# First attention's softmax sums by 32x32 transposes on VectorE, and three weight requests at other steps

## What is computed

```python
qkv = x @ Wqkv.T;  scores = causal(q @ k.T / sqrt(128))
x = layernorm(x + (softmax(scores) @ v) @ out_w.T)
# second: Q, K with scaled columns, V from x @ Wa; the same softmax; @ Wp
x = layernorm(x + attn2(x) @ Wp)
```

## Time and profile before

| | us |
|---|---|
| median of 3 runs | 1966.73 |
| lowest | 1963.15 |
| the profiled execution | 1965.32 |
| its span on the slowest core (6) | 1963.8 |
| first attention, head 0 to the final matmuls (core 6) | about 97 to 573 |
| second attention with its projections | about 790 to 1725 |
| TensorE, VectorE, ScalarE, GpSimd busy | 1907.4, 1135.3, 965.5, 253.9 |

### The profile page before, as it was taken

One profiled execution on the slowest core, in us unless ns is written; L12 is line 12 of the kernel. 1 busy time (PEld: TensorE's weight loads), 2 busy tenths in 40 slices (PEclk: granted clock), 3 DMA queues, 4 the chain that ended last, 5 costly groups with the idle time before them and its releaser, 6 DMA issues.

```text
span 1963.8 us, 30387 instructions; the slowest of 8 cores (1951.1 to 1963.8 us)
## 1 busy us (share of the span) xinstructions
PE 1907.4 (97%) x10286; PEld 992.5 (51%) x10286; DVE 1135.3 (58%) x1976; ACT 965.5 (49%) x1333; POOL 253.9 (13%) x372
## 2 busy tenths in 40 slices
PE   5999999999999999999999999999999999889997
PEld 2445445544444444555647465564746556334443
DVE  0288889988953644145556556555565655524333
ACT  0288888888853433144453545445354444622221
POOL 3011111111122441001010001100000000100000
PEclk9999999999999999999999999999999999999999
DMA  9712121221487996132121322212122220593642
GB/s 144 125 33 57 41 65 41 58 49 39 87 163 138 274 280 167 41 55 54 34 49 31 62 44 55 54 33 51 34 58 44 54 44 17 84 201 107 224 184 86
DMA packets 91271, 170.01 MB, mean 87 GB/s; under 512 B 39544, under 2 KB 58096, under 8 KB 81904
## 3 DMA queue, kind: packets, MB, share of 16 engines
q1 hardware_dynamic: 61936, 107.77, 19.4%
q0 software_dynamic: 28896, 59.77, 19.3%
q10 hardware_dynamic: 288, 0.52, 0.1%
HBM read 185.62 MB, written 33.80 MB: 112 GB/s over the span
## 4 chain that ended last, share of the span: by engine, by line
PE 92%; DMA 4%; ACT 1%; DVE 1%; issue 1%; POOL 1%; DVEq 0%; ACTq 0%; POOLq 0%; SPq 0%
PE pj L319 32%; PE c_ps L671 11%; PE s_ps L441 11%; PE pj L1149 11%; PE s_ps L951 11%; PE pj L951 5%; PE c_ps L951 3%; PE l_ps L951 3%; DMA bufA<-wp 2%; DMA bufB<-xT 2%; PE l_ps L576 1%; PE s_ps L823 1%; PE pj L406 1%; ACT pt L453 0%; PE pj L650 0%
## 5 line engine op out<-in xcount | busy, mean ns | idle before, releaser
L453 ACT ACTIVATE pt<-s_ps,mbias 128x1024 bf16<-128x1024 f32 (+2 forms) x640 | 630.7, 988 | 465.9 <-PE s_ps L441 390.2
L319 PE MATMUL pj<-bufA,ws 128*128 128x512 bf16 x2048 | 479.9, 379 | 1.0 <-DVE z L974 1.0
L671 PE MATMUL c_ps<-pt,v 128*128 128x512 bf16 (+3 forms) x1280 | 341.9, 349 | 5.7 <-ACT cf L685 4.0
L319 PEld LDWEIGHTS pj<-bufA,ws 128*128 128x128 bf16 x2048 | 198.3, 98 | 230.9 <-issue 3.8
L510 DVE TENSOR_TENSOR acc<-acc,pt 128x1024 f32<-128x1024 f32 x180 | 219.8, 1221 | 69.8 <-ACT pt L453 65.5
L319 PE MATMUL pj<-bufB,ws 128*128 128x512 bf16 x896 | 243.5, 379 | 0.1
L1149 PE MATMUL pj<-wv,bufA 128*128 128x256 bf16 x2048 | 238.3, 273 | 0.0
L461 POOL TENSOR_SCALAR_AFFINE_SELECT pt<-pt 128x256 bf16<-128x256 bf16 x256 | 124.7, 489 | 872.3 <-ACT pt L453 857.5
L1149 PEld LDWEIGHTS pj<-wv,bufA 128*128 128x128 bf16 x2048 | 199.4, 98 | 37.5 <-issue 0.3
L979 ACT ACTIVATE sqs<-z 128x512 f32<-128x512 f32 x128 | 80.5, 629 | 240.0 <-DVE z L974 230.9
L671 PEld LDWEIGHTS c_ps<-pt,v 128*128 128x128 bf16 x1280 | 124.2, 98 | 141.9 <-issue 19.6
(11 more groups left out here) (141 smaller groups left out, 1857.1 us busy)
## 6 DMA issues: line engine op xcount, KB each, us to landing
rb<-rr_res SPq DMA_DIRECT2D x116, 256.0 KB, 3.8
ws<-wqk POOLq DMA_DIRECT2D x32, 512.0 KB, 6.3
z<-x SPq DMA_DIRECT2D x16, 1024.0 KB, 6.5
x_res<-z SPq DMA_DIRECT2D x16, 1024.0 KB, 7.6
z<-x_res SPq DMA_DIRECT2D x16, 1024.0 KB, 6.5
out<-z SPq DMA_DIRECT2D x15, 1024.0 KB, 7.4
bufB<-xT POOLq DMA_DIRECT2D x16, 512.0 KB, 39.3
bufB<-wo POOLq DMA_DIRECT2D x4, 2048.0 KB, 25.6
```

The lines of the kernel that those rows point to most:

```text
L319: tok = P.pe(lambda t, c=c, b=b: t.matmul(pj[b][:, :], lhs(c), rhs(c), start=(c == 0), stop=(c == NCH - 1)), waits=wt, inc=(c == NCH - 1))
L453: self.exp_tok[g] = P.ac(lambda s: s.activation(pt[:, 0:n], sp[:, 0:n], AF.Exp, bias=mbias[h % 2][:, :]), waits=[self.s_tok[g], self.mb_ok ...
L671: last = t.matmul(c_ps[:, q0:q0 + n], self.vbuf(h)[:, c * 128:(c + 1) * 128], pt[:, o:o + n], start=(beg and n_ == 0), stop=(end and n_ == 1))
```

## The change

Attention 1 gets a scratch tile `tr1` in the room of a hi and a lo tile, and is built with `turned` set, so that it goes through `turn`, `lsum_turned` and the short `recip`. `split_hi`, `split_lo`, `lsum` and the long reciprocal are deleted. In attention 1, `lsum_turned` comes at step 23, that is step 3 of the next head; the reciprocal stays at step 4 of the next head. Where attention 1 calls `sums` (before `feed`) is kept, now by the flag `fold_out`.

The copy that begins window 0 in attention 1 moves from VectorE to ScalarE. The last head's windows 2 and 3 of attention 1 are copied from PSUM to the room of `acc`, not to the ring `cf`. Quarters 1, 2 and 3 of Wp are requested at steps 4, 8 and 12.

```diff
-    hi1 = [row("hi1_0", 36864, 512, BF16), row("hi1_1", 24576, 512, BF16)]
-    lo1 = [row("lo1_0", 37888, 512, BF16), row("lo1_1", 25600, 512, BF16)]
+    tr1 = row("tr1", 36864, 512, F32)
...
                 if kind == "a":
-                    t1 = P.ve(lambda v: v.tensor_copy(src, pt[:, 0:512]),
-                              waits=[ok, self.src_read[0]] +
-                              ([] if self.fold_out else [self.fold_ok[NW - 1]]))
+                    if self.fold_out:
+                        t1 = P.ac(lambda s: s.copy(src, pt[:, 0:512]),
+                                  waits=[ok, self.src_read[0]])
+                    else:
+                        t1 = P.ve(lambda v: v.tensor_copy(src, pt[:, 0:512]),
+                                  waits=[ok, self.src_read[0], self.fold_ok[NW - 1]])
...
                 free = [self.cf_free[m]] if m is not None else \
-                    [self.turn_ok, self.norm_tok[(H - 3, NW - 1)]]
+                    [self.turn_ok, self.fold_ok[NW - 1], self.norm_tok[(H - 3, NW - 1)]]
...
         def add_up(self, g, n, todo):
-            for what, hh, w in todo:
-                if what == "split" and not self.turned:
-                    self.split_hi(w)
             if g + 1 < n:
                 self.sums(g + 1)
             for what, hh, w in todo:
                 if what == "split":
-                    (self.turn if self.turned else self.split_lo)(w)
+                    self.turn(w)
...
     at1 = Att("a1", 0, lambda h: kT, lambda h: q1[h % 2], lambda h: v1, bufA, pt1, acc1, f1,
-              True, hi1, lo1, cf1, rb1, None, r41, (3, 7, 13, 21), (8, 10, 15, 23), 4,
-              (6, 7, 8, 12), (10, 12, 14, 16))
+              True, [], [], cf1, rb1, None, r41, (3, 7, 13, 21), (0, 0, 0, 23), 4,
+              (6, 7, 8, 12), (10, 12, 14, 16), tr1,
+              [None, None] + [row(f"cl1_{i}", 32768 + 2048 * i, 512, F32) for i in range(2)])
...
-    at2.at_step[(H - 1) * NST + 7] = lambda tok: wp_tok.append(
-        load_big(bufA, wp_d, 1, [x2_end[0], tok]))
-    at2.at_step[(H - 1) * NST + 13] = lambda tok: wp_tok.extend(
-        load_big(bufA, wp_d, i, [x2_end[0], tok]) for i in (2, 3))
+    for n, ew in ((4, 1), (8, 2), (12, 3)):
+        at2.at_step[(H - 1) * NST + n] = lambda tok, ew=ew: wp_tok.append(
+            load_big(bufA, wp_d, ew, [x2_end[0], tok]))
```

More of the change, by code:

```diff
@@ L527, in sums @@
                                        waits=[t] + ([self.src_read[1]] if self.fold_out else []))
-        def split_hi(self, w):
-            src, _ = self.sources(w)
-            hi = self.hi[w % len(self.hi)]
-            self.hi_ok[w] = P.ac(lambda s: s.copy(hi[:, :], src),
-                                 waits=[self.fold_ok[w], self.hl_free[w % len(self.hi)]])
-        def split_lo(self, w):
-            src, n = self.sources(w)
-            hi, lo = self.hi[w % len(self.hi)], self.lo[w % len(self.hi)]
-            self.lo_ok[w] = P.ve(lambda v: v.tensor_sub(lo[:, :], src, hi[:, :]),
-                                 waits=[self.hi_ok[w], self.fold_ok[w],
-                                        self.hl_free[w % len(self.hi)]])
-            self.src_read[n] = self.lo_ok[w]
         def turn(self, w):
@@ L564, in lsum_turned @@
             self.hl_free[0] = self.l_tok[h]
-        def lsum(self, h, w):
-            hi, lo = self.hi[w % len(self.hi)], self.lo[w % len(self.hi)]
-            def mm(t):
-                last = None
-                for half in (0, 1):
-                    n = 2 * w + half
-                    band = strip[:, 112 - 16 * n:240 - 16 * n]
-                    for src in (hi, lo):
-                        last = t.matmul(l_ps[:, 0:256], band, src[:, half * 256:half * 256 + 256],
-                                        start=(n == 0 and src is hi),
-                                        stop=(n == 2 * NW - 1 and src is lo))
-                return last
-            self.l_tok[h] = P.pe(mm, waits=[self.hi_ok[w], self.lo_ok[w], tok_strip] +
-                                 ([self.r_tok.get(h - 1), bank_free[7]] if w == 0 else []))
-            self.hl_free[w % len(self.hi)] = self.l_tok[h]
         def recip(self, h):
@@ L593, in recip @@
                 return
-            self.r_tok[h] = P.ve(lambda v: v.reciprocal(self.r4[:, 0:256], l_ps[:, 0:256]),
-                                 waits=[self.l_tok[h], self.ro_tok.get(h - 1)])
-            self.ro_tok[h] = P.dma(
-                "sync", f"{self.tag}ro",
-                rr_d[self.row0 + h, :, :].rearrange("w (a c) -> (w a) c", a=2),
-                self.r4[0:128:16, 0:256], waits=[self.r_tok[h]])
         def rbuf(self, h, w):
@@ L731, in run @@
                 todo = plan.get(g, [])
-                if not self.turned:
+                if self.fold_out:
                     self.add_up(g, n, todo)
@@ L743, in run @@
                 self.feed(target(h, i))
-                if self.turned:
+                if not self.fold_out:
                     self.add_up(g, n, todo)
@@ L748, in run @@
                 for what, hh, w in todo:
-                    if what == "lsum" and not self.turned:
-                        self.lsum(hh, w)
-                    elif what == "lsum":
+                    if what == "lsum":
                         self.lsum_turned(hh)
```

## The result

The change made the kernel slower by 0.2%: ratio 1.0022, interval 1.0013 to 1.0031. The median of 14 executions is 1970.7 us (lowest 1966.5) against 1965.6 (lowest 1963.1) for the kernel before in the same series of runs. Some executions of each kernel, 6 of the 14 of the changed one, ran in a slower state of the chip, and the ratio is of the others alone, whose median is 1968.5 us for the changed kernel. The forecast was 1961, with a range that holds 1970.7, but it had the sign wrong: some 4 us more came where some 4 less were forecast. The profiled execution of after took 1966.5 us, the shortest of the 14.

A forecast was written before the change was run, and what follows sets the result against it. The prediction took TensorE as the first attention's bound, VectorE 10% under it, and late Wp weights as the final projection's stall. It summed 1965.3 + 1.0 (first attention) - 5 (Wp requests) to 1961 us, range 1950 to 1975.

The forecast's parts named there:

- The bound changes hands: First attention: VectorE, needing 30.35 us a head, replaces TensorE as the bound, whose need falls from 30.4 to 28.7.
- The price on VectorE: First attention: 4.8 us of VectorE work go out and 6.7 come in, net +1.9 us a head.
- The waits that remain: First attention: VectorE as the bound still waits 0.4 us a head, giving period 30.75 and +2.7 us over 13 periods.
- The row of 530 to 545 us: Head 14 of the first attention: VectorE busy 14.02 of 15 us, 0.5 us of waits; source of the 0.4 a head.
- cost 0: First attention, window 0 copy moved to ScalarE: the exponential queued behind it delays nothing; without that cover 1.3 us a head.
- Head 0, head 14, tail: First attention outside the 13 periods: head 0 -1.3 us, head 14 +0.6, tail -1.0 from the shorter reciprocal.
- the hole of 75 GB/s at 1704 to 1708: DMA traffic before the final projection: filling it with earlier Wp requests is worth 2 to 4 us, 3.5 taken.
- the limit of 39 us: Whole kernel: a 2% change in time, about what a measurement can tell from none; slower 0.03, faster 0.02, same 0.95.
- B: First attention: TensorE stays the bound, added VectorE work fits into its waits, 28.7 to 29 us a head; 1938 us, chance 0.07.
- A: First attention: VectorE keeps 2.09 us of waits a head and TensorE's clock falls after stalls; 1983 us, chance 0.15.
- C: Final projection: earlier Wp requests change nothing, bandwidth alone sets quarter 2's landing; -1 us or so, 1965, chance 0.2.
- D: Final projection: the Wp stall goes wholly, 9 us, with VectorE never waiting in the first attention; 1952 us, chance 0.13.

The follow-up runs named there:

- the run with late normalisations: Kernel before with Wp requests at steps 4, 8, 12 and head 14's products in attention 2's last head at steps 8, 10, 13, 15: ratio 1.0005.

## Why the prediction went wrong, point by point

The forecast was +1.0 us for attention 1 and -5 for the requests. Alone, the attention measured +5.7 and the requests -2.2. So both terms failed, the attention's by 4.7 us and the requests' by 2.8.

**The bound changes hands: right.** TensorE is busy for 94.8% of the stretch (382.10 of 403.08), VectorE for 92.2%, and TensorE stands for results that hang on VectorE. Taking 2.7 us a head from VectorE shortened the period by 1.27.

**The price on VectorE: right.** Forecast 28.45 + 1.9 = 30.35 us a head; measured (403.08 - 10.0) / 13 = 30.24, so 1.8 were added. The durations taken from attention 2 hold: 703 for the transpose, 686 for the sum, 343 for the reciprocal.

**The waits that remain: the failed step in attention 1.** Forecast 0.4 us a head, measured 10.0 / 13 = 0.77, which alone is 13 x 0.37 = 4.8 us; less 1.4 for the smaller need, that is 3.4, and core 0's stretch of 403.1 is 3.3 over the forecast of 399.8 (the median core's 402.5 is 2.7 over). The row of 530 to 545 us was the right kind of row, but it was read from a kernel in which the copy was on VectorE. With the copy there the waits are 4.9 / 13 = 0.38, just the forecast value, but the need is 30.79, so that the forecast period of 30.75 is met in neither kernel. The forecast gave the copy on ScalarE "cost 0" and so took its move as a saving of 0.6 us a head; the saving that remains is 0.15. It argued from ScalarE's 328 of 397 us, an average. That ScalarE stands 1.0 us for the mask in the diagonal steps, with the exponential of the next step behind it, is measured; that this makes VectorE's waits is the likely reason and not shown.

**Head 0, head 14, tail: 1.7 us of gains that didn't come.** Head 14 was forecast at +0.6 and came at +0.4 and +0.6. The tail stayed at 20.5 us to the tenth, so the shorter reciprocal in front of the early tile sat on no path. For head 0 the first reciprocal moves by -0.8 us on the later and -0.3 on the earlier cores, and its medians lie between 122.0 and 126.8 in all kernels with either head 0: a gain of 1.3 can't be seen, nor excluded. In all attention 1 and its tail cost 5.7 us instead of 1.0.

**Wp: the failed step in the requests.** The forecast read the hole of 75 GB/s at 1704 to 1708 as room, "which goes on beside the four broadcasts of reciprocals". It filled the hole with quarter 1, which was to bring quarter 2 forward by 3.5 us, and priced the early tile and the mask as the only ones that could suffer. Both halves of that failed. Quarter 2 came forward by nothing on the later cores (55.8 us after the last short reciprocal before and after) and by 0.7 on the earlier ones. And the broadcasts suffered. They then took a median of 11.6 us instead of 6.3, and the first reader stands in VectorE's in-order stream ahead of the reciprocal for which TensorE waits: +4.1 and +4.2 us in the last head. The row of the hole says itself that there was less room than its GB/s suggest: the share of the DMA engines is 0.76 there, against 1.13 with the full queue. The Trainium skill (DMA: Bandwidth & Descriptors, Queues, rings and completion order) says that each DMA engine serves its queues in turn by packets. By that rule a second 2 MB transfer beside them slows the broadcasts though they are on SyncE's queue; the trace shows the later landing, and no run here shows the order of the packets. A hole still stands in after, with 100 GB/s and a share of 0.77 at 1709 to 1713 on core 0, where the broadcasts now are, so the early request didn't fill it, and what makes it stays open.

The size of the stall was right by luck: forecast 2.8, measured 2.43 on core 0, and -5.9 us in the final part of the later cores where -5 was forecast. But the stall fell because TensorE came 4.1 us later and not because the weights came sooner, and with the last head at its old length the stall is back at 6.1 us (the run with late normalisations). On the later cores the two together are -5.9 + 4.1 = -1.8 us, on the earlier ones, which had 1.9 to 2.7 us to win, -2.5 + 4.2 = +1.7.

**Sum.** By the stages the later cores change by -0.8 + 5.7 + 0.4 + 4.1 - 5.9 = +3.5 us, and their spans by +4.2; the sums of medians don't close better than that. The forecast spoke of even and odd cores as if the odd ones were early by nature; they were so in one execution. The slowest core went from 1963.8 to 1964.9 in the profiled executions; the ratio of the runs is 0.22%, or 4.3 us.

**Small sums.** For the requests the forecast's own numbers give 2.8 + 1.7 = 4.5 us left of 8.9 (6.34 + 2.57), so -4.4 and not -5. Four quarters of 2 MB at 148 GB/s from 1688.2 end near 1745 and not 1747. And neither case named for the limit of 39 us reaches it: 3 us of waits a head are 13 x (33.35 - 30.54) = +36.5 us before the gains of 1.7 and 5, and B with all of Wp is -21 - 1.7 - 9 = -32.

**Rivals.** A fell: VectorE's waits for the mask were 7.8 us, not 20.8, and the clock stayed at 1.00 in the 13 heads, so that its price of a stall in each head was never put to the test. B fell: 1.8 us didn't fit into 2.1 of waits. C came nearest for the requests: it said -1 us, they gave -2.2, and its reason, that bandwidth sets the landing, is what the landings show. D is seen on single cores (no stall for Wp on cores 1, 2, 4, 5 and 6) and shows that the stall's end isn't a gain by itself.

## What to carry to other kernels

When work moves to an engine that is within 10% of the bound, its price can be read well from rows of the same operation elsewhere, to 0.1 us in 1.9 here; the waits that remain can't be read from a stretch in which another engine still has a job that the change moves, and an engine's average load doesn't say that an instruction which stands behind a wait costs nothing.
A transfer that is asked for earlier doesn't land earlier for that: compare its landing, counted from a fixed instruction, before you credit a shorter stall to it, for a reader that comes later sees a shorter stall too.
A hole in the DMA traffic is not free room if small transfers run in it: before asking for a large one earlier, list the small ones in flight, and follow each to its reader and to what stands behind that reader in order.
With unequal cores, compare those that ended late with those that ended late, whatever their number, and never count two halves as averaged between two engines until a run shows that a surplus is carried over.

## What the runs showed of the hardware

**The mask on GpSimd slows beside VectorE's additions.** The same instruction on core 0, before and after, from 126 to 524 us:

```profile
L461 POOL TENSOR_SCALAR_AFFINE_SELECT pt<-pt 128x256 bf16<-128x256 bf16 x104 | 56.0, 542 | 318.3 <-ACT pt L453 304.2 <-PE c_ps L671 12.2
```

```profile
L460 POOL TENSOR_SCALAR_AFFINE_SELECT pt<-pt 128x256 bf16<-128x256 bf16 x103 | 83.4, 813 | 299.6 <-ACT pt L452 286.3 <-PE c_ps L635 10.7 <-PE pj L318 1.3
```

It grows from 542 to 813 ns, and was 703 with the copy on VectorE. Single ones in after's timeline:

```profile
339.37 0.69 DVE L515 TENSOR_TENSOR acc<-acc,pt 128x512 f32<-128x512 f32 x1 [0.43 <-POOL pt L460]
339.58 0.74 POOL L460 TENSOR_SCALAR_AFFINE_SELECT pt<-pt 128x256 bf16<-128x256 bf16 x1 [0.38 <-PE c_ps L635]
...
347.66 0.40 POOL L460 TENSOR_SCALAR_AFFINE_SELECT pt<-pt 128x256 bf16<-128x256 bf16 x1 [6.83 <-ACT pt L452]
347.81 1.32 DVE L512 TENSOR_TENSOR acc<-acc,pt 128x1024 f32<-128x1024 f32 x1
```

The first mask starts inside an addition and takes 0.74 us; the second starts ahead of one and takes 0.40, and the addition takes 1.32 where 1.23 is its mean. The timelines of the 13 heads on core 0 say the same of all masks: in after 84 of 104 begin inside a VectorE instruction with two inputs, and these take 0.90 us on the mean; before it was 68, with 0.61. The other masks take 0.40 to 0.47 us on the mean. VectorE's busy share alone doesn't say how long a mask takes: with the copy on VectorE it is the higher one, 376.01 of 405.17 us (92.8%, against 92.2% in after), and the mask is the shorter one, 703 ns.

**Neighbouring cores don't get their weights alike.** With the requests early and the normalisations late, one core of each pair of neighbours ends 8 to 10 us ahead of the other:

```profile
core 0: 1958.7 us, clock 0.994
core 1: 1948.8 us, clock 0.998
core 2: 1949.2 us, clock 0.995
core 3: 1958.2 us, clock 0.993
```

In the profiled execution of before it was the odd one in each pair; here it is core 1 and core 2, then 4 (1951.5) and 7 (1949.4). It goes together with the stall on Wp, 5.2 to 6.3 us on the later and 1.0 to 1.9 on the earlier cores, and with the landing of quarter 2, which is at 54.9 to 56.1 us after the last short reciprocal on the later and at 50.4 to 51.3 on the earlier ones. It looks as if two neighbours share what brings the weights; no run tested that.
